# Attention and routed experts on one core: the iterations written out, and ScalarE masking two of the four routing heads

## What is computed

```python
# attention, 16 heads of 16, 64 features each
qp = relu(q @ rw) + eps;  kp = relu(k @ rw) + eps
kv = sum over rows of kp * v           # one state per sequence
out = (qp @ kv) / (qp @ sum(kp) + eps) @ Wo + bo
x = layernorm(x + out)
# FFN: a dense part and 1024 experts of one vector each, picked by product keys
sx, ixx = top_k(q_x @ keys_x, 8);  sy, ixy = top_k(q_y @ keys_y, 8)   # 4 heads
scores, pk = top_k(sx[:, None] + sy[None, :], 8);  idx = all_ix[pk]
w = silu(x . down_embed[idx]) * softmax(scores)
y = (silu(x @ Wg + bg) * (x @ Wu + bu)) @ Wd + bd + sum_k w_k up_embed[idx_k]
x = layernorm(x + y)
```

## Time and profile before

| | |
|---|---|
| median of 3 runs | 4005.03 us (4003.9 to 4014.2) |
| the profiled execution's own time | 4021.45 us |
| its span, first to last instruction | 4019.7 us |
| TensorE clock granted, mean | 0.966 |
| PE, DVE, POOL, ACT busy | 3759.8, 3012.2, 1686.0, 1347.7 us |
| instructions | 58160 |

### The profile page before, as it was taken

The page is one execution under the profiler, slowest core; times in us unless marked ns, Lnnn a source line. Parts: engine busy times, 40 slices in busy tenths (PEclk is TensorE's granted clock), DMA queues, the critical chain, the costliest instruction groups (busy, mean ns, idle before and its releaser), DMA issues.

```text
span 4019.7 us, 58160 instructions
## 1 busy us (share of the span) xinstructions
PE 3759.8 (94%) x19388; PEld 3133.7 (78%) x19388; DVE 3012.2 (75%) x5947; ACT 1347.7 (34%) x1990; POOL 1686.0 (42%) x1004
## 2 busy tenths in 40 slices
PE   8878999999999999999999999999999999888888
PEld 7757888888787887878788777888877788776776
DVE  2277887777787777877777778777778777888883
ACT  3223333233333333333333333333333333332321
POOL 0044444344443444544344444434444444544541
PEclk7668999999999999999999999999999999999999
DMA  3000000000000000000000000000000000000000
GB/s 106 6 11 11 16 17 11 12 17 11 17 16 17 11 11 17 11 17 17 12 11 16 12 16 17 17 12 11 17 12 17 17 6 11 11 11 7 11 6 11
DMA packets 23384, 61.75 MB, mean 15 GB/s; under 512 B 5552, under 2 KB 10032, under 8 KB 23088
## 3 DMA queue, kind: packets, MB, share of 16 engines
q1 hardware_dynamic: 18480, 41.04, 3.0%
q0 software_dynamic: 4608, 16.78, 1.0%
HBM read 41.04 MB, written 16.78 MB: 14 GB/s over the span
## 4 chain that ended last, share of the span: by engine, by line
PE 70%; DVE 11%; issue 9%; POOL 6%; ACT 4%; DVEq 0%; ACTq 0%; SPq 0%; POOLq 0%; DMA 0%
PE ring L549 19%; PE y_bank L633 9%; PE y_bank L635 8%; POOL grid L391 5%; PE rt_bank L549 4%; PE at_bank L572 4%; PE kv_bank L521 4%; DVE grid L957 4%; PE at_bank L492 3%; PE kv_bank L492 3%; PE at_bank L478 2%; PE kv_bank L516 2%; PE at_bank L563 2%; PE pt_bank L613 2%; PE kv_bank L484 2%
## 5 line engine op out<-in xcount | busy, mean ns | idle before, releaser
L391 POOL TENSOR_TENSOR grid<-ex 128x1024 f32<-128x1024 f32 x512 | 1242.5, 2434 | 527.6 <-ACT ex L755 198.7
L957 DVE SCALAR_TENSOR_TENSOR grid<-grid,best 128x1024 f32<-128x1024 f32 x512 | 703.4, 1374 | 105.6 <-POOL grid L391 104.7
L972 DVE SCALAR_TENSOR_TENSOR prob<-grid,rz,prob 128x1024 f32<-128x1024 f32 x384 | 651.1, 1696 | 8.3
L633 PE MATMUL y_bank<-wd_sb,gate 128*128 128x256 f32 x2048 | 624.1, 387 | 5.3 <-DVE wexp L994 5.3
L635 PE MATMUL y_bank<-up_sb,wexp 128*128 128x256 f32 x2048 | 611.6, 380 | 0.0
L382 POOL TENSOR_SCALAR qp<-qp 128x512 f32<-128x512 f32 x256 | 231.6, 905 | 565.9 <-ACT qp L746 559.8
L549 PE MATMUL ring<-x1T_hl,wg_hl 128*128 128x512 f32 x1536 | 430.0, 416 | 41.2 <-issue 39.2
L549 PE MATMUL ring<-x1T_hl,downT_hl 128*128 128x512 f32 x1536 | 423.9, 412 | 20.8 <-ACT gate L760 20.8
L635 PEld LDWEIGHTS y_bank<-up_sb,wexp 128*128 128x128 f32 x2048 | 391.1, 191 | 53.0
L549 PE MATMUL ring<-x1T_hl,wu_hl 128*128 128x512 f32 x1536 | 428.2, 415 | 0.0
L633 PEld LDWEIGHTS y_bank<-wd_sb,gate 128*128 128x128 f32 x2048 | 356.2, 192 | 47.4 <-issue 19.5
(11 more groups left out here) (122 smaller groups left out, 5825.1 us busy)
## 6 DMA issues: line engine op xcount, KB each, us to landing
xb<-in_L_attn_x SPq DMA_DIRECT2D x34, 512.0 KB, 3.5
out_y<-x POOLq DMA_DIRECT2D x32, 512.0 KB, 3.0
xa<-in_L_attn_x SPq DMA_DIRECT2D x30, 512.0 KB, 3.5
prob<-in_L_ffn_down_embed SPq DMA_DIRECT2D x1, 1024.0 KB, 5.9
prob<-in_L_ffn_Wg SPq DMA_DIRECT2D x1, 1024.0 KB, 8.7
prob<-in_L_ffn_Wu SPq DMA_DIRECT2D x1, 1024.0 KB, 10.5
wd_sb<-in_L_ffn_Wd SPq DMA_DIRECT2D x1, 1024.0 KB, 11.4
up_sb<-in_L_ffn_up_embed SPq DMA_DIRECT2D x1, 1024.0 KB, 11.9
```

Source lines behind the costliest of these rows:

```text
L391: pool.tensor_tensor(grid[:, h % 2], bcast(ex[:, h, 0:NX].unsqueeze(2), [P, NX, NK]), bcast(ex[:, RH + h, 0:NK].unsqueeze(1), [P, NX, NK]) ...
L633: pe.matmul(rows, gate[:, c % 2, t * P:(t + 1) * P], wd_sb[:, c, :], start=(c == 0 and t % 2 == 0), stop=False, skip_group_check=True)
L957: marks["keep", h] = rt_steps.mark(dve.scalar_tensor_tensor(out=g, in0=g, scalar=best[:, h, TOP - 1:TOP], in1=g, op0=ALU.is_ge, op1=ALU.mult))
L972: ins = dve.scalar_tensor_tensor(out=row, in0=g, scalar=rz[:, h:h + 1], in1=row, op0=ALU.mult, op1=ALU.add, accum_out=mass[:, 0:1] if h == ...
```

## The change

Two edits. First, `schedule` writes all iterations 4 to 38 out, on every engine; no loop and no register value is left. Second, heads 0 and 1 of each tile are masked by ACT. DVE's `choose` makes two more small vectors, `drop` = minus the eighth best product and `lift` = the eighth best product times `rz`. ACT then does, for a head, a Prelu of grid + `drop` with slope 2^30 on the negative side, which leaves kept entries at or above 0 and throws the others far below, and a Relu of `rz` times that + `lift`, which gives `rz` times the kept product and 0 for the others. Head 0 goes to `prob`, head 1 stays in its grid buffer, and DVE adds the two with one plain addition in place of `keep` 0, `keep` 1, `add` 0 and `add` 1. Heads 2 and 3 stay as they were.

```diff
+    ACT_HEADS, STEEP = 2, float(2 ** 30)
...
-            with eng.Fori(2, B) as b:
-                with eng.Fori(0, BG // 2) as j:
-                    for par in range(2):
-                        step(b * BG + j * 2 + par, par, b)
-                batch_end(b)
...
+            for it in range(BG, NG + LAST_LAG):
+                if it <= NG and it % BG == 0:
+                    batch_end(it // BG - 1)
+                live = [0 <= it - lag < NG for lag in (0, ATTN_LAG, ROUTE_LAG, FFN_LAG, LAST_LAG)]
+                body(it, it % 2, *live, it // BG)
... POOL, spread
-                    wait(pool, rt_dve, s * RT_STEPS + (t - (h < 2)) * len(RT_TILE) + RT_AT["add", (h - 2) % RH])
+                    if h == 2:
+                        pool.wait_ge(masked, s * (ACT_HEADS * T) + t * ACT_HEADS + 1)
+                    else:
+                        wait(pool, rt_dve, s * RT_STEPS + (t - (h < 2)) * len(RT_TILE) + RT_AT["add", (h - 2) % RH])
... ACT
+                def mask(t, h):
+                    act.wait_ge(spread_ready, s * (RH * T) + t * RH + h + 1)
+                    act.wait_ge(rt_dve, s * RT_STEPS + t * len(RT_TILE) + RT_AT["lift"])
+                    g = grid[:, h].rearrange("p a b -> p (a b)")
+                    act.activation(g, g, ACT.Prelu, bias=drop[:, h:h + 1], alpha=STEEP).then_inc(bent, 1)
+                    if t == h == 0:
+                        wait(act, pt_full, (s - 1) * C)
+                    act.wait_ge(bent, s * (ACT_HEADS * T) + t * ACT_HEADS + h + 1)
+                    act.activation(prob[:, other, t, :] if h == 0 else g, g, ACT.Relu, scale=rz[:, h:h + 1],
+                                   bias=lift[:, h:h + 1]).then_inc(masked, 1)
...
                     if ff:
                         ff_gate(c)
+                    if rt and c % 2:
+                        mask(c // 2, 0)
...
                             kv_use(main, in_main(a), *use)
+                    if rt and c % 2:
+                        mask(c // 2, 1)
                     if ff:
                         ff_dots(c)
... DVE, choose
+                    rt_steps.mark(dve.tensor_scalar(drop[:], best[:, 0:ACT_HEADS, TOP - 1], -1.0, None, ALU.mult))
...
+                    rt_steps.mark(dve.tensor_tensor(lift[:], best[:, 0:ACT_HEADS, TOP - 1], rz[:, 0:ACT_HEADS],
+                                                    ALU.mult))
... DVE, add_head
+                    if h < ACT_HEADS:
+                        dve.wait_ge(masked, s * (ACT_HEADS * T) + t * ACT_HEADS + ACT_HEADS)
+                        ins = dve.tensor_tensor(row, g, row, ALU.add)
... DVE, the order of a stage
-                    if rt and c == 1:
-                        add_head(t, 0)
-                    if rt and odd:
-                        keep(t, 1)
...
-                    if rt and odd:
-                        add_head(t, 1)
                     if rt and odd:
                         keep(t, 2)
...
                     if ff:
                         ff_wexp(c)
                     if rt and odd:
-                        add_head(t, 2)
+                        add_head(t, 1), add_head(t, 2)
...
-                    if rt and not odd:
-                        keep(t, 0)
-                    if rt and not odd and c:
-                        add_head(t, 0)
```

More of the change, by code:

```diff
@@ L118, in block_kernel @@
         best = sb("best", P, RH, TOP)
-        zsum, rz = sb("zsum", P, RH), sb("rz", P, RH)
+        narrow = sb("narrow", P, 16)
+        zsum, rz, mass = narrow[:, 0:4], narrow[:, 4:8], narrow[:, 8:10]
+        drop, lift = narrow[:, 10:12], narrow[:, 12:14]
         grid = sb("grid", P, 2, NX, NK)
         prob = sb("prob", P, 2, T, NEXP)
-        mass = sb("mass", P, 2)
         gate = sb("gate", P, 2, G)
@@ L160, in block_kernel @@
         spread_ready, prob_ready = sem("spread_ready"), sem("prob_ready")
+        bent, masked = sem("bent"), sem("masked")
         ring_full, ring_act = sem("ring_full"), sem("ring_act")
@@ L169, in block_kernel @@
         AT_STEPS = 2 * T + 2 * T
-        RT_TILE = (["top", "less", "cand", "best", "sum", "rz"]
-                   + [(step, h) for h in range(RH) for step in ("keep", "add")] + ["mass"])
+        RT_TILE = ["top", "less", "cand", "best", "drop", "sum", "rz", "lift", ("keep", 2), ("add", 1),
+                   ("add", 2), ("keep", 3), ("add", 3), "mass"]
         RT_AT = {name: k + 1 for k, name in enumerate(RT_TILE)}
@@ L266, in schedule @@
         def schedule(eng, body, batch_end):
-            def step(it, par, batch=None):
-                live = lambda lag: not isinstance(it, int) or 0 <= it - lag < NG
-                body(it, par, live(0), live(ATTN_LAG), live(ROUTE_LAG), live(FFN_LAG), live(LAST_LAG), batch)
-            batch_end(0)
-            for it in range(BG, 2 * BG):
-                step(it, it % 2, it // BG)
-            batch_end(1)
-            with eng.Fori(2, B) as b:
-                with eng.Fori(0, BG // 2) as j:
-                    for par in range(2):
-                        step(b * BG + j * 2 + par, par, b)
-                batch_end(b)
-            with eng.Fori(0, BG // 2) as j:
-                for par in range(2):
-                    it = j * 2 + (NG + par)
-                    body(it, par, False, True, True, True, True, B)
-            for it in range(NG + BG, NG + LAST_LAG):
-                step(it, it % 2, it // BG)
+            for it in range(BG, NG + LAST_LAG):
[3 more added lines that the diff above has]
+                body(it, it % 2, *live, it // BG)
         PREP_STEPS, PREP_WG, PREP_WU = 11, 9, 10
@@ L735, in body @@
                 a, m, s, n = it, it - ATTN_LAG, it - ROUTE_LAG, it - FFN_LAG
+                other = 1 - par
                 def at_use(kind, j):
@@ L951, in choose @@
                     marks["rz"] = rt_steps.mark(dve.reciprocal(rz[:], zsum[:]))
+                    rt_steps.wait()
+                    rt_steps.mark(dve.tensor_tensor(lift[:], best[:, 0:ACT_HEADS, TOP - 1], rz[:, 0:ACT_HEADS],
+                                                    ALU.mult))
                 def keep(t, h):
@@ L963, in add_head @@
                     row = prob[:, other, t, :]
-                    rt_steps.wait(marks["keep", h])
-                    if h == 0:
-                        rt_steps.wait(max(marks["rz"], marks["keep", h]))
-                        if t == 0:
-                            wait(dve, pt_full, (s - 1) * C)
-                        ins = dve.tensor_scalar(row, g, rz[:, 0:1], None, ALU.mult)
+                    if h < ACT_HEADS:
+                        dve.wait_ge(masked, s * (ACT_HEADS * T) + t * ACT_HEADS + ACT_HEADS)
+                        ins = dve.tensor_tensor(row, g, row, ALU.add)
                     else:
-                        rt_steps.wait(marks["add", h - 1])
+                        rt_steps.wait(max(marks["keep", h], marks["add", h - 1]))
                         ins = dve.scalar_tensor_tensor(out=row, in0=g, scalar=rz[:, h:h + 1], in1=row,
@@ L1025, in body @@
                     uses(KV_FIRST[c])
-                    if c == 1:
-                        uses(AT_EARLY[c])
-                    if rt and c == 1:
-                        add_head(t, 0)
-                    if rt and odd:
-                        keep(t, 1)
-                    if c != 1:
-                        uses(AT_EARLY[c])
+                    uses(AT_EARLY[c])
                     if ff:
```

## The result

| | before | changed |
|---|---|---|
| median | 4009.61 us (4003.9 to 4015.53, 4 runs) | **4072.2 us** (4069.46 to 4076.41, 4 runs) |
| ratio to before | | **1.0157**, 95% interval 1.0136 to 1.0178 |
| span of the profiled execution | 4019.7 us | 4074.6 us |
| TensorE clock granted, mean | 0.966 | 0.959 |

The change makes the kernel 1.6% slower. The forecast of 4005 us, no change, was wrong; the time lies inside the range of 3940 to 4080.

The account below looks back on a forecast made before the run. PE, busy for 94% of the span, was taken as the bound. Writing out the iterations (-88 us) and the masks on ACT (+88 us) summed to 0, so 4005 us, no change; range 3940 to 4080.

Parts of the forecast that it names:

- Edit 1, -88: All iterations written out: 75.5 us from 23 shorter steps plus 12 us from the drain's edges; bounds 49 and 96.
- template of 115.6 us: Step from iteration 6 to the already written-out iteration 7, taken as every step's length, against 118.9 us in the loops.
- DVE's relief, 3.7 us a tile: DVE loses two masks, a scaling and part of an addition, gains two tiny vectors: 470 us less in all.
- Stage 1, "the stop changes place: 0 us": PE starts `qp` 0 1.7 us late but no longer stops ahead of the k product: 0 us, bounds 0 and 1.7.
- Stage 3, +2.1: Later grids and mask 3 delay DVE's division, so PE starts `qp` 6 2.1 us later; bounds 1.1 and 2.7.
- Stage 7, +0.5: `norm1` may wait for POOL's grid 3 and make PE 0.5 us late; bounds 0 and 0.9.
- Stage 5, 0.1: ACT has only two Silus and two copies, DVE no division behind its mask: 0.1 us.
- Sum per step, 2.7: The masks' cost to PE over all stages, 2.7 us in each of iterations 6 to 31, 70 us.
- Drain, +18: Iterations 32 to 35, k and v part over, stage 1's 1.7 us not made up: 4.4 us each, 18 us.
- ACT's queue becomes PE's: Rival, chance 0.18: stage 1's 1.7 us not repaid, stage 3 at its upper end, 5.3 us in 30 iterations: 4076 us.
- Only the branches' stops come back: Rival, chance 0.10: writing out gains only 49 us, the stops at the loops' branches: 4044 us.
- the hold-ups stay hidden: Rival, chance 0.27: POOL's grid 3 meets no DVE pass, `norm1` keeps its reserve, masks cost 40 us: 3957 us.

Follow-up runs that it names:

- experiment 1: Kernel before with its iterations written out, nothing else changed: 3932.45 us, ratio 0.9816; second measurement 3917.73 us, 0.978.
- experiment 9: Changed kernel with the changes of experiments 3, 4 and 7 together: 3892.49 us, ratio 0.9701 to the kernel before.
- experiment 4: Changed kernel with `drop` made by a negated DVE reduction and `lift` by tiny ACT passes: 4025.82 us, ratio 1.0031.
- experiment 7: Kernel of experiment 3 with DVE's division of `qkv` 1 put ahead of mask 3 in stage 3: 3946.42 us, ratio 0.9837.
- experiment 3: Changed kernel with head 0's two ACT passes behind the early reading of q instead of ahead: 4007.21 us, ratio 0.9995.
- experiment 5: Changed kernel with stage 1's down-projection made twice on PE, the second for nothing, at its stop: 4046.22 us, ratio 1.0111.

## Why the forecast was wrong

The gain of edit 1 came about as forecast; the step that failed is the cost of edit 2, put at 88 us and measured at about 138. Three of its terms carry the miss: the clock, for which there was no term (about 1 us a step), `drop` and `lift`, priced at 0.18 us each and measured at 1.0, and stages 1 and 5, put at 0 and 0.1 us and measured at 0.4 and 0.56.

Where the 55 us between the spans come from, by the gate Silus that open the iterations:

| us | before | 1 | changed | 9 |
|---|---|---|---|---|
| up to iteration 6 | 329.3 | 317.2 | 330.6 | 316.3 |
| iteration 6 | 115.3 | 115.4 | 120.1 | 114.9 |
| iterations 7 to 31 (25) | 2967.2 | 2886.1 | 2993.6 | 2881.4 |
| iterations 32 to 36 | 529.8 | 528.1 | 548.7 | 496.9 |
| from 37 on | 78.1 | 78.0 | 81.6 | 81.2 |

- **Edit 1, -88: right**, -74 and -88 in two measurements. The template of 115.6 us was met by 115.4. Not met were the 12 us of the drain's edges: iterations 32 to 36 took 528.1 and 522.9 us against 529.8. The bound by the branches' named stops, 49 us, fell. Iterations 7 to 30 took 80 us longer in the loops. Of these the stops at the branches are 36 (11 of the 12 stops of the earlier trace rows); 15 more are other stops of PE that the written-out kernel doesn't have, 7.4 ahead of `qp` 6, 6.6 ahead of stage 7's down-projection, waiting for ACT's `gate`, and 1.2 ahead of a `next` transpose; 37.5 us of half clock, each time at the end of a stop at a branch or right behind it, account for up to half of their length, 19; some 10 us of longer matmul time I can't name.
- **Masks, passes of ACT and its sum: right** to 2%.
- **DVE's relief, 3.7 us a tile: wrong.** The failed term is "two tiny vectors of about 0.18, as that of `rz`". They took 2.0 us together in the mean. 123 of 128 `drop` and 77 of 128 `lift` began while POOL multiplied a grid, and ended within 0.03 us of that grid's end; alone they took 0.17 and 0.16 us. Another 24 `lift` began within 0.005 us of a grid's start and took 160 ns; two more began as close and were held for 1.91 us. The reciprocal beside them, whose row I took as the price, was never held (177 to 180 ns, 74 times inside a grid product), nor was the sum (175 to 178 ns in experiment 4, 123 times inside one). I had priced by size; here the kind of operation and the neighbor decide.
- **Stage 1, "the stop changes place: 0 us": half right.** The stop did go from k to `qp` 0, it was 2.25 us instead of 1.7 (the held `drop` is in it), and the step lost 0.4 to 0.5 us. Wrong was that a stop that changes place costs nothing: at its new place it is 2.25 us long instead of 1.66, and the granted clock falls behind it in nearly every second iteration. This adds 1.1 us to the mean step, the two stops of 4.0 us included. The forecast had no term for the clock at all.
- **Stage 3, +2.1: right** (+1.9, experiment 7 gives back 1.6). **Stage 7, +0.5: right.** **Stage 5, 0.1: wrong**, 0.56 us. About 0.36 of it are the held `drop` and `lift` again: in iteration 9 they took 1.04 and 1.52 us on DVE ahead of the division of `qkv` at the start of stage 5, which ended 0.5 us later than in experiment 1, and PE's weight load for the next use of the attention bank waited for it (`PEld at_bank L564 <- DVE x L912: 22.4, 32, 3.8`; in experiment 1 two such waits, 2.3 us). With experiment 4's forms this wait is gone and stage 5 takes 15.0 us. So the term that was mis-sized reaches PE, in a stage that was put at almost nothing. The other 0.2 us stand ahead of a product of the k/v bank.
- **Sum per step, 2.7: wrong**, 3.3 at full clock and 4.3 in the mean, 104 us over 24 steps instead of 65. Of the 39 us by which it fell short, 25 are the difference of mean and short step, the half clock (21) and the two held `lift` of stage 1 (3.5), for which the forecast had no term; the other 14 are stages 1 and 5, less what stage 3 saved.
- **Drain, +18: near**, 20.6 or 25.8 us, depending on which measurement of experiment 1 is taken. The cause given, stage 1's lateness that nothing repays, is not all of it: experiment 3 takes 12 of them back (536.5 us), and experiment 4 takes 22 by the form of `drop` and `lift` alone.
- **From 37 on**, for which the forecast had no term: +3.6 us. Up to iteration 6 the table shows +13, but the two measurements of experiment 1 differ by 9 there, with 164 and 140 us at half clock; how much of it is the masks' stays open.

So edit 2 cost about 138 us instead of 88, within its bounds of 40 to 159, and the forecast missed by that; edit 1, by its first measurement, adds up to 14. Of the rivals, "ACT's queue becomes PE's" gave 4076 us, and its number is near; its reason was another. It had stage 1's 1.7 us lost and stage 3 at its upper end; neither happened. Experiment 3 shows that the pair ahead of q's reading cost 2.2 of the 4.3 us a step, and nearly half of this came through the clock; experiment 5 takes 0.7 us a step back by work in the stop alone. "Only the branches' stops come back" fell with experiment 1, "the hold-ups stay hidden" with the steps of 118.7.

The rule of the Trainium skill that I weighed ("ScalarE: Activation LUTs", rules for kernel authors) ends up on neither side. It would keep these masks on VectorE; as written, the change bore it out, but experiment 9 has them on ACT and is 0.6% to 1.0% faster than either measurement of the written-out kernel, by the medians. At 1143 and 1243 ns against DVE's 1374 ns, place in the queue decided and not speed per element.

## What to carry to other kernels

When a pass moves to another engine, look first at what stands behind it in that engine's queue and who waits for it: an exchange of two blocks was worth 65 us here, as much as the whole change had lost. Price a small instruction by the same kind of operation beside the same neighbors, not by its size. And ask of a stop of the engine that bounds the kernel what the clock does behind it: the stop of 2.25 us in stage 1 cost more than its length, because the half clock followed it in every second iteration, while no stop of up to 1.7 us there had this effect. Judge an engine's relief stage by stage, because what is paid back in the steady state can be worth something in the drain.
